# One full-array product in place of four quarters for the scan's first product, with a block-diagonal ring of keys filled by small DMAs

## The reference

```
v_old  = einsum('bhd,bhde->bhe', k_t, state)
delta  = clip(v_t - v_old, -1, 1)
update = clip(0.9 * k_t[..., :, None] * delta[..., None, :], -1, 1)
state  = state + update          # scaled by 0.9 where a state exceeds 10
o      = clip(einsum('bhij,bhj->bhi', state, q_t), -1, 1)
```

## Time and profile before

| what | value |
|---|---|
| median of 3 runs | 1384.04 us (1383.59 to 1386.72) |
| profiled execution, its own time | 1393.87 us |
| span of its profile | 1392.1 us |
| PE matmul, busy | 1243.0 us, 89% |
| PE weight load | 813.5 us, 58% |
| DVE | 1000.2 us, 72% |
| ACT | 820.1 us, 59% |
| POOL | 910.7 us, 65% |
| mean granted TensorE clock | 0.929 of full speed |

### The profile page before, as it was taken

The page is one execution under the profiler, slowest core; times in us unless marked ns, Lnnn a source line. Parts: engine busy times, 40 slices in busy tenths (PEclk is TensorE's granted clock), DMA queues, the critical chain, the costliest instruction groups (busy, mean ns, idle before and its releaser), DMA issues. The chain is left out here.

```text
span 1392.1 us, 47171 instructions
## 1 busy us (share of the span) xinstructions
PE 1243.0 (89%) x18561; PEld 813.5 (58%) x18561; DVE 1000.2 (72%) x4437; ACT 820.1 (59%) x2193; POOL 910.7 (65%) x1321
## 2 busy tenths in 40 slices
PE   7777797989999998998899999999999999998896
PEld 3333454656566575756656665755666565757654
DVE  3768878778777868787786888978888775464432
ACT  2232253556676576757476666657574657667764
POOL 5353668686968677685776676776857466674541
PEclk8687678989999999999999999999999999999998
DMA  6000101001000000000010000100001010101000
GB/s 175 2 1 5 30 12 31 24 15 28 12 20 19 16 21 11 24 15 19 14 27 12 15 24 8 29 8 23 15 6 32 6 39 10 34 15 31 4 3 7
DMA packets 27257, 29.35 MB, mean 21 GB/s; under 512 B 12146, under 2 KB 22291, under 8 KB 27027
## 3 DMA queue, kind: packets, MB, share of 16 engines
q0 software_dynamic: 8336, 16.73, 4.9%
q1 hardware_dynamic: 18690, 9.51, 2.5%
HBM read 24.90 MB, written 2.29 MB: 20 GB/s over the span
## 5 line engine op out<-in xcount | busy, mean ns | idle before, releaser
L1873 POOL DMA_INDIRECT sb<-table,sb x240 | 241.8, 1007 | 81.5 <-issue 51.1
L1041 DVE TENSOR_TENSOR_SCAN ps<-ps,sb 128x47 f32<-128x47 f32 (+3 forms) x1024 | 271.0, 265 | 30.5 <-ACT sb L1445 1.5
L1033 DVE TENSOR_TENSOR ps<-sb,ps 128x24 f32<-128x24 f32 (+3 forms) x1024 | 193.1, 189 | 14.7
L541 PE MATMUL ps<-sb 128*128 128x512 bf16 x585 | 177.6, 413 | 8.7 <-ACT sb L1658 2.7
L1733 POOL TENSOR_TENSOR sb<-sb 128x1 f32<-128x1 f32 x128 | 73.2, 574 | 138.3 <-DVE sb L976 137.6
L610 PEld LDWEIGHTS ps<-sb 32*32 32x32 f32 x2032 | 41.0, 108 | 107.6 <-DVE sb L1013 65.6
L610 PE MATMUL ps<-sb 32*32 32x32 f32 x2032 | 69.8, 209 | 36.2 <-DVE sb L1013 35.6
L621 PEld LDWEIGHTS ps<-sb 32*32 32x32 f32 x2032 | 41.5, 108 | 93.1 <-DVE sb L1049 54.3
L982 DVE TENSOR_TENSOR sb<-ps,sb 128x128 f32<-128x128 f32 x112 | 32.2, 289 | 80.5 <-PE ps L708 29.8
L541 PEld LDWEIGHTS ps<-sb 128*128 128x128 bf16 x585 | 54.7, 105 | 58.8 <-issue 14.5
L1369 ACT ACTIVATE sb<-ps 128x128 f32<-128x128 f32 x128 | 34.9, 275 | 90.7 <-PE ps L564 90.2
(11 more groups left out here) (313 smaller groups left out, 3532.3 us busy)
## 6 DMA issues: line engine op xcount, KB each, us to landing
sb<-table,sb POOLq DMA_INDIRECT x240
sb<-in_cs SPq DMA_DIRECT2D x16, 128.0 KB
table<-sb SPq DMA_DIRECT2D x17, 64.0 KB, 1.5
sb<-dscr SPq DMA_DIRECT2D x64, 2.0 KB
out<-sb SPq DMA_DIRECT2D x16, 64.0 KB, 1.6
sb<-in_x SPq DMA_DIRECT2D x3, 256.0 KB, 5.4
sb<-in_wex SPq DMA_DIRECT2D x1, 512.0 KB, 4.1
sb<-in_rvx SPq DMA_DIRECT2D x1, 512.0 KB, 4.5
```

What stands on the lines that cost most here:

```text
L541: e.matmul(b[:, 0:512], onesb[:, :], onesb[:, :].unsqueeze(1).to_broadcast([128, 4, 128]), start=True, stop=True)
L1033: e.tensor_tensor(at(psP, p + ROW - 3 - 2 * m, [ROW, 3], [2, m], [1, 2]), AC[:, row(n, k), :, HIST - 2 * m:HIST].rearrange("p r (a b) -> p ...
L1041: e.tensor_tensor_scan(at(psD, 16 + k + COMB * skip, [COMB, 3 * ROW - skip]), at(psP, p + skip, [1, 3 * ROW - skip]), Q[:, i % 32, skip:3 ...
L1873: e.indirect_dma_start(GA[:, k, :], None, table[0:128 * i + 128, :] if i else table0, bass.IndirectOffsetOnAxis(u[:, k:k + 1], 0)).then_in ...
```

## The change

The four quarter products become one product of the whole 128 x 128 array. Its weights are `KZB`, a new buffer of 8 slots (a ring) of 128 x 128, one slot for a block, with the four 32 x 32 squares of keys on the diagonal and zeros elsewhere. The zeros are written once, by a POOL memset in the prep stage. The keys get there by DMAs that SyncE issues: a new `front` stage on SP has 4 steps for a chunk, each of which fills 4 slots (one half of the ring, for 4 blocks) with 8 DMAs, one for each half of each quarter. One such DMA moves 4 partitions by 4 blocks by 32 fp32: 16 rows of 128 bytes.

```
 # PE, scan
-                    w.wait_ge(*f.V2.at("kz", c))
-                    for q in range(4):
-                        rows = slice(32 * q, 32 * q + 32)
-                        x = e.matmul(psS[rows, 0:32], KZT[c % 2][rows, 32 * o1:32 * o1 + 32], R[g % 2][rows, :],
-                                     start=g == 0, stop=True, skip_group_check=True)
-                    x.then_inc(sc.p, 1)
+                    w.wait_ge(*f.D2[g // 4 % 2].at("kb", g // 8))
+                    e.matmul(psS[:, 0:32], KZB[:, g % 8, :], R[g % 2][:, :], start=g == 0, stop=True,
+                             skip_group_check=True).then_inc(sc.p, 1)
 # DVE, front: before it turns KZ to KZT
-            w.wait_ge(sc.p, 16 * (c - 1))
+            w.wait_ge(*f.D2[1].at("kb", 2 * (c - 2) + 1))
 # POOL, prep
+            e.memset(KZB[:, :, :], 0.0).then_inc(*PG("zk"))
 # SP, front
+            for j in range(4):
+                G = 4 * c + j
+                to = slice(4 * (G % 2), 4 * (G % 2) + 4)
+                yield
+                w.wait_ge(*f.V2.at("kz", c))
+                w.wait_ge(*PG.at("zk", 0))
+                w.wait_ge(sc.p, 4 * (G - 1))
+                for q in range(4):
+                    for u in range(2):
+                        rows = slice(32 * q + 16 * u + 12, 32 * q + 16 * u + 16)
+                        e.dma_start(KZB[rows, to, 32 * q:32 * q + 32],
+                                    KZT[c % 2][rows, 128 * j:128 * j + 128].rearrange("p (o k) -> p o k", k=32)).then_inc(*f.D2[G % 2]("kb"))
 # the order of SP's steps: f is a fill
-        "ppppmpppmpppmppmpppmppppmppppmppmppppmpmpppppmpmpppmppepemeppppmpeepemeeeeeeeeee",
+        "pfffffffffpfppfmffpfffppmfffpfppmfffpfpmpfffpfpmpfffpppfmfffpffppffpmfppfmffpfppfffpmffpmpfpffppfffpmffpmfpf"
+        "pffpmfpfpefpemeppppmpeepemeeeeeeeeee",
```

More of the change, by code:

```diff
@@ L308, in _program @@
     PP, PA, PV, PG = ev("prep_P", ["pw0", "pw1", *CEN]), ev("prep_A", ["pw0", "pw1", "bt", *CEN]), ev("prep_V", ["ez", "eps", "b1", "kg", "zK", "zZ", "zD", "zP", "bP", "q1", "q2", "q3", "q4", "nk", "ns", "zb", "lb", "ub", "zq"]), \
-        ev("prep_G", ["bz", "zo", "zr", "n100", "hf", "z0", "z1", "hb", "b1", "b2", "b3", "zl", "v0", "v1", "one"])
+        ev("prep_G", ["bz", "zo", "zr", "zk", "n100", "hf", "z0", "z1", "hb", "b1", "b2", "b3", "zl", "v0", "v1", "one"])
     PD = ev("prep_D", ["zrow"], 16)
@@ L333, in _program @@
     f.A2, f.P2 = ev("front_A2", ["kT", "kp", "k0", "k2", "v0", "v2", "z0", "z2", "kn"]), ev("front_P2", ["kv"])
-    f.V2 = ev("front_V2", ["kz"])
+    f.V2, f.D2 = ev("front_V2", ["kz"]), [ev(f"front_D2{k}", ["kb"] * 8, 16) for k in range(2)]
     f.D = ev("front_D", ["qk", "v"], 16)
@@ L341, in _program @@
     KZ = sb([128, 16, 32])
+    KZB = sb([128, 8, 128])
     g_ = Stage()
```

## The result

| | before | after |
|---|---|---|
| median, same chip | 1389.01 us (1383.17 to 1398.24, 20 runs) | 1399.34 us (1389.20 to 1410.18, 20 runs) |
| ratio, 95% interval | | 1.0081 [1.0061, 1.0100] |
| profiled execution, its span | 1393.87, 1392.1 us | 1394.96, 1393.1 us |

The changed kernel is slower by 0.8%; 1380 was forecast. Of the 19 us between 1380 and 1399, 5 are the starting point: the median of 3 runs was 1384.04, that of 20 is 1389.01. Against the kernel before, -4 us was forecast and +10 measured. The two profiled executions are 1 us apart, one from the upper half of its kernel's runs, the other from the lower half of its own. So the loss has to be sought in stages.

A forecast was written before the change was run, and what follows sets the result against it. It took the long middle to be close to TensorE's own pace, with a reserve; TensorE -5, VectorE +1, first fill +0.3, POOL +1 and -1.3 for short bf16 weights made -4 us: 1384.04 to 1380.0, range 1371 to 1392.

The forecast's parts named there:

- The product on TensorE: First product, line 610: one full-array product replaces the quarters' way in and out, -5 us, bounds -16 and +4.
- VectorE's side: VectorE's wait for the first product at line 1049: result later or earlier by block, +1 us, between -6 and +4.
- rival 2: Line 1049: the longer product decides, 0.15 us later where VectorE has no room, 1392 us; chance 0.13.
- rival 3: First product: packing was worth it, quarters' way in and out is paid anyway by the second product, 1391 us; chance 0.07.
- The fills: 512 DMAs on SP, 0.6 us each, a fill ready 7.3 us after its condition: cost 0, bounds 0 and +45 us.
- Rival 4: Fills late, from 1.3 us an issue on or a landing above 7 us: 1395 to 1430 us; chance 0.08.
- What the fills push on SyncE: Palette steps on SP: loads move by 4 to 5 us, +2.5 us on POOL, +1 on the span, at most +3.
- signs of being wrong: Line 1049's wait grows; TensorE waits for fills; POOL waits at line 1840 in several chunks; line 621's way in grows.
- First fill: Block 0's product waits for it: ready at 27.05 against a start at 27.26, cost 0 to +2 us, taken as 0.3.
- memset: POOL's prep step: zeroing 128 x 1024 takes 1 us at about 9.4 us, nothing close behind, cost 0.

The follow-up runs named there:

- x2_product_again: Changed kernel with the ring filled only for the first eight blocks and SyncE's order of before, measured again: 1.0037 of before, faster kind.
- after_fifth: The changed kernel unaltered, measured again as yardstick of its call: 1.0087 of before, faster kind.
- x1_cs_ahead: Kernel before's four quarters kept, with the fills, the changed order and the load of in_cs issued earlier: 1.0048 of before, faster kind.
- eight_small: Changed kernel with all eight transfers of each fill, from the third on, cut to one row of one block: 0.9982 of before, slower kind.
- one_of_eight: Changed kernel with only the first of each fill's eight transfers from the third fill on: 0.9895 of before, slower kind.
- act_copies: Changed kernel with ScalarE copying the keys into the ring, no transfers, SyncE's order of before: 0.9926 and 0.9936 of before, slower kind.
- cs_ahead: Changed kernel with SyncE's load of in_cs issued as soon as its buffer is free: 0.9943 of before on the slower kind, 1.0032 on the faster.
- before_again: The kernel before, unaltered, measured again against itself: 1.0004, slower kind.

## Why the prediction was wrong, step by step

**The product on TensorE, -5 us.** The mechanism was right: the way into and out of the quarters goes. Its size between 128-column products was too small, 0.144 us a block and not 0.06, and 0.09 between bf16 ones. I had taken a product of eight columns between others of eight, 0.23 from one to the next; between 128 columns the new product's two weight loads run from 568.09 to 568.39, beside its neighbours' matmuls, and it adds 0.14 to a plain step. Against the quarters it costs 0.15 more between narrow products (0.14 forecast), 0.05 more behind one (0.03), and the same ahead of one (0.06 less). All together, TensorE's saving is of the size forecast: 4.1 us in the 129 blocks counted above, 5.4 less busy over the run. (The bounds of this term, -16 and +4, don't come out of what is named there: -5 less 118 x 0.08 is -14, -5 and 7 is +2.) On the slower kind the product alone brings 0.8%, 10 to 12 us. On the faster kind, the one of the forecast, it has the other sign: +0.4%, 5 us. This is the first step that failed: TensorE's saving was counted as time (-4 us with VectorE's side), and no gain at all came of it on this kind.

Part of that shows in the granted clock. Over the runs beside x2_product_again the time falls by 7.2 us for each 0.01 of mean granted clock (a straight line through the runs, one level for each kernel); before has 0.933 on the mean, the product alone 0.929, so some 3 us go with the clock, and 1.1 us, with a standard error of 1, remain at equal clock. That is not told from nothing. The change with the load ahead, in the same runs, has 0.932: 0.9 us go with the clock and 4.2, with a standard error of 0.9, remain. So the near equal ratios of the two (1.0037, 1.0032) need not be one and the same loss. For the change itself, in the runs of after_fifth, it is 0.928 against 0.933 with 8.1 us per 0.01: 4.4 us by the clock, 6.7 at equal clock. Of the 7 us of the late load, then, only some 2.5 are there at equal clock (6.7 less 4.2, with a standard error of 1.4), and the rest goes with the clock, as in the stretch above. That the clock falls because TensorE has less to do is an argument, not shown: no run put dummies in for the time saved. What keeps TensorE's saving from becoming time on the faster kind, and what the versions with a filled ring lose at equal clock, stays open.

**VectorE's side, +1 us.** In order as far as it can be seen: the wait at the mask fell by 5 us (38.1 to 33.3), where rival 2 had it grow. Rival 2 gave 1392 and rival 3 1391, both nearer to 1399 than I was, but not by their mechanisms: the quarters are not cheaper than the full product between full-array steps, only beside narrow ones, and the "issue" before the second product didn't grow (30.8 us before, 28.5 after).

**The fills, 0.** The issues took 0.64 us each (forecast 0.6), a fill 5.4 to 5.9 us (4.8). None was late: the trace has no wait of TensorE for a transfer at L610. The last issue of the first fill ended 1.2 us ahead of its product, that of every other at least 6 us ahead. This is L2014 after (ns min/median/max, first and last start):

```profile
L2014 SPq DMA_DIRECT2D sb<-sb x512: 637/637/818, 19.1 to 1097.7; - x171
```

Rival 4 was not it. In the changed kernel with the load ahead the ratios show no cost of the fills: 1.0032 against the product's 1.0037 on the faster kind, and on the slower kind 0.9943 against 0.9917, whose intervals overlap. A cost of some us isn't excluded: it shows at equal clock (above), with the quarters (x1_cs_ahead), and on the slower kind, where the stretch has 5 of the 12 us by which eight_small is behind one_of_eight.

**What the fills push on SyncE, +1 us, at most +3.** The second step that failed, and the one that costs most. The place was right to the chunk: the load found at 991.7 with a fill ahead of it, reader held, GpSimd's list behind it. I priced it at GpSimd's wait, 2.5 us, and let 1 us of it pass, at most 3. The wait was 4.5 us, since GpSimd got there at 992.4 and no longer at 996.4 as in the earlier trace rows, the scan being ahead by then; and I didn't look whose operations stand behind the reader. They belong to another stage, TensorE waits for them with the scan's product behind, and all of the wait passed to VectorE (4.3 us); the stretch lost 7.4 us, with the clock at 1.2 GHz behind the wait, and the time 7. One of the signs of being wrong came true here: GpSimd waited at this line in two chunks, for 2.0 and 4.5 us.

**First fill +0.3, memset 0.** First product at 26.0 us in place of 27.3: no cost.

**By sum**, on the faster kind: +5 for the product where -4 was forecast, +7 for the load where +1 was, 0 for the transfers: 12 us above before, and 10 to 12 measured. The +7 is the difference of two of the measured ratios, so that the sum closes is no check of its own.

No version beat both kernels on both kinds of chip. On the slower one act_copies and cs_ahead did, by 0.6 to 0.7% against before; on the faster the kernel before stays the fastest.

## What to carry to other kernels

A step put into an in-order queue is priced by what stands behind it, and then by what stands behind the reader of that: follow the chain through each engine's list until it meets the engine that sets the pace, above all where the reader shares its queue with another stage. Look too at the clock behind a wait of TensorE: here the wait was 4.3 us and the stretch lost 7.4. A small transfer isn't free where it is one of many: its 0.64 us on the issuing queue counts, not its bytes; and a load that would stand behind such a fill should go out ahead of it (for chunk 12 it did by some 60 us). Time saved on the busiest engine is a forecast only for the chip on which the saving was seen, since the same edit gave -0.8% on one kind and +0.4% on the other.

## What the runs showed of the hardware

- Two kinds of chip, one program: before takes 1386 to 1389 us on three chips (with the one of the forecast) and 1454 to 1459 on three others. Its mean granted clock is 0.93 on the faster kind and 0.91 on the slower. On the slower kind TensorE has more "issue", and the profiles have waits put down to "remote", to no engine or DMA of the core (20 to 39 us in all in each of the twelve, most on ScalarE and VectorE). None of the eight profiles of the faster kind has one; such rows in before_again:

```profile
PEld ps L610 <- issue: 40.4, 74, 1.5
...
ACT sb L1670 <- remote: 10.7, 2, 9.0
...
DVE sb L1049 <- remote: 2.4, 3, 1.9
```

  All "issue" ahead of TensorE's matmuls adds up to 31.6 us there and to 6.5 in before on the chip of the forecast. Why chips differ is not known. The changed list has 3048 fewer TensorE instructions (1524 matmuls and as many weight loads), and 138 packets in place of 149 for q8, the queue that brings instructions. That this is why the product gains on that kind fits these rows and is not shown apart.
- A transfer of 128 bytes made 32 packets (496 such and 16 full ones: 34882 - 18690 = 16192), more than one of 16 rows of 128 bytes (20: 10240 for 512).
- On both kinds the time goes with the mean granted clock of the run, 6.5 to 8.2 us for each 0.01.
- Behind a wait of 3.0 to 4.3 us in the scan the clock was at 1.2 GHz for 6.8 or 10.2 us, in seven profiles of seven.
